# Attention loop on one Trainium2 core: the tile whose scores stay in PSUM is put first in each group of four, on TensorE and ScalarE

## The chip, the cores and the metric

The kernel runs on one core of a Trainium2 chip. The metric is the device time of one execution in microseconds (us); lower is better. The times below are the median of three executions. The profile and the trace come from one further execution, whose own time is given beside its span.

## The reference

Only the attention matters here. For four batches, sixteen heads, 1024 positions and a head dimension of 8:

```python
q, k, v = (heads(q), heads(k), heads(v))
scores = jnp.einsum('bhqd,bhkd->bhqk', q, k) * scale
scores = scores + _tisa_bias(amplitudes, sharpness, offsets, s)[None]
weights = jax.nn.softmax(scores, axis=-1)
attn = jnp.einsum('bhqk,bhkd->bhqd', weights, v)
out = attn.transpose(0, 2, 1, 3).reshape(b, s, d)
```

The bias depends on the head and on the distance between key and query, not on the batch. Ahead of it stand a layer norm and the projection to q, k and v; behind it a gated output projection, a residual, a second layer norm and a small feed-forward layer in 8-bit numbers.

## The kernel before

The attention is one loop over 8 pairs of heads (`Fori(0, NH2)`, index i). Each pass holds 16 **groups** g (2 heads times 8 blocks of 128 keys), written out one after the other. A group has four **tiles**, one for each batch b. A tile is 128 keys by 1024 queries of scores. So the loop has 128 groups, 512 tiles. Three engines share the work of a tile, and each runs its own instructions strictly in the order in which they are written; semaphores tie the engines together.

Names used from here on, for group g and tile b:

- **S_b** is the matmul pair (two halves of the queries) of the scores on TensorE, line 1043. For b = 0, 1, 2 the result lands in one of two pairs of PSUM banks, used in turn (`unit(k)`, with k = 3g + b counting these tiles). For b = 3 it lands in the one pair of banks 4 and 5.
- **T** follows S_3 alone: four matmuls (line 1052) add the bias to the scores where they lie in PSUM. Tile 3 is the tile that stays in PSUM; VectorE never touches it.
- **z_b** is VectorE's addition (line 1118), b = 0, 1, 2 only: PSUM plus bias, into a buffer in SBUF. It counts up `z_ready`.
- **e_b** is ScalarE's exponential (line 1170 for b = 0, 1, 2, in place in the SBUF buffer; line 1178 for b = 3, from PSUM to the buffer). It counts up `p_ready`.
- **P0 and P1** are TensorE's products of the group's four exponentials with the values, one for each half of the queries (line 1068; each shows as 8 matmul records, two passes over four column strips).

Who waits for whom: z_b waits for S_b; S_b of the tiles 0 to 2 waits until the addition two tiles earlier has emptied its banks (`z_ready` at k - 1); e_b waits for z_b, e_3 for T. P0 of group g waits for all four exponentials of g. S_3 of group g waits, before the change, for `p_ready` at 4 g, which is all four exponentials of group g - 1. TensorE computes scores two groups ahead of the products (`LAG = 2`), four sets of SBUF buffers hold the groups in flight, and the order in which TensorE takes the pieces of one step is a table in the loop:

```python
for steps, c in (((0,), 0), ((1,), 1), ((2, 3), None)):
    ...
        for b in steps:
            scores(i, g + LAG, b)
    ...
    if c is not None:
        products(i, g, c)
```

So in step g TensorE runs S_0 of group g + 2, P0 of g, S_1 of g + 2, P1 of g, S_2 and S_3 with T of g + 2. ScalarE takes the tiles of each group in the order 0, 1, 2, 3. Once in each pass of the head pairs, in group 1, VectorE and ScalarE each also copy one half of the finished output out of PSUM (lines 400 and 401), and in group 3 VectorE takes a reciprocal.

Of the kernel before, what the change touches and what calls it, by code (L numbers as in the profile page):

```python
# [30 lines left out]
B, S, D = 4, 1024, 128  # L31
# [29 lines left out]
ROW = 64  # L61
ROW2 = 16
EARLY = (H - 2) * HD
PAIR = 2
RING = [2, 3, 4, 5, 6, 7]
NLN = 5
# [2 lines left out]
def attention_block(nc, io, out):  # L69
    with ExitStack() as ctx:  # L70
# [22 lines left out]
        win = sb("win", [P, 3 * D], F32)  # L93
        wgate = sb("wgate", [EARLY + 1, 2 * D], F32)
        wlast = sb("wlast", [P, 2 * D], F32)
# [296 lines left out]
        p_ready = sem("p_ready")  # L392
        num_in = [sem(f"num_in{b}") for b in range(B)]

        GPH = TB
# [34 lines left out]
        def gate_main(eng, i):  # L430
# [3 lines left out]
            if i >= len(RING):  # L434
                eng.wait_ge(prod_ready, i - len(RING) + 1)
            for m in range(PAIR):
                t = PAIR * o + m
                eng.matmul(gate_ps(i)[:, m * 2 * D:(m + 1) * 2 * D], num[b][0:EARLY + 1, t * P:(t + 1) * P],  # L438
                           wgate[:, :], start=(m == 0), stop=True, skip_group_check=True)
# [15 lines left out]
        with nc.Block() as block:  # L455
            @block.sync
            def _(eng):
# [8 lines left out]
                eng.dma_start(wffn[:, :], io["w_ffn"]).then_inc(consts_in, 16)  # L466
                eng.dma_start(wgate[0:EARLY, :], io["w_gate"][0:EARLY, :]).then_inc(consts_in, 16)
                eng.dma_start(wgate[EARLY:EARLY + 1, :], io["b_gate"].rearrange("(a n) -> a n", a=1)).then_inc(consts_in, 16)
                for b in range(B):
                    eng.dma_start(wlast[32 * b:32 * b + 2 * HD, :], io["w_gate"][EARLY:P, :]).then_inc(consts_in, 16)  # L470
                with nc.allow_non_contiguous_dma(reason="128 biases, one per partition"):
# [475 lines left out]
            def _(eng):  # L947
# [29 lines left out]
                with eng.Fori(0, NH2) as i:  # L977
# [13 lines left out]
                    with eng.If(i > NH2 - 2):  # L991
# [3 lines left out]
                        for b in range(B):  # L995
                            eng.dma_start(num[b][0:EARLY, :], o_dram[b, 0:H - 2]).then_inc(num_in[b], 16)
                            eng.dma_start(num[b][EARLY:EARLY + 1, :], rd[HD + 1:HD + 2, :]).then_inc(num_in[b], 16)
# [24 lines left out]
            @block.tensor  # L1022
            def _(eng):
                def scores(i, g, b):

                    p, t = (g // GPH) % 2, g % GPH
                    by_vector = b < DPG
                    if b == 0 and t == 0:
                        eng.wait_ge(head_in[p], (i + (g // (2 * GPH))) * (16 * LOADS) + 16 * LOADS)
                    if by_vector:  # L1030
                        k = DPG * g + b
                        u = unit(k)

                        if k >= 2:
                            eng.wait_ge(z_ready, i * (2 * DPH) + (k - 1))
                    else:
                        u = 4
                        if g:
                            eng.wait_ge(p_ready, i * (8 * GPH) + 4 * g)
                    keys = slice(b * S + t * P, b * S + (t + 1) * P)  # L1040
                    for c in range(2):
                        rows = slice(ROW * c, ROW * c + 33)
                        last = eng.matmul(ps[:, u + c, :], kb[p][rows, keys],  # L1043
                                          qb[p][rows, b * HALF:(b + 1) * HALF],
                                          start=True, stop=True)
                    if by_vector:
                        last.then_inc(sd_ready, 1)
                        return
                    for c in range(2):
                        for m in range(2):  # L1050
                            c0 = t * P + 64 * m + c * HALF
                            last = eng.matmul(ps[64 * m:64 * m + 64, u + c, :], ident2[:, :],  # L1052
                                              t64[p][:, c0:c0 + HALF], start=False, stop=True,
                                              skip_group_check=True)
                    last.then_inc(sp_ready, 1)

                def products(i, g, c):

                    p, t = (g // GPH) % 2, g % GPH
                    if c == 0:  # L1060
                        eng.wait_ge(p_ready, i * (8 * GPH) + 4 * (g + 1))
                        if t == 0:
                            eng.wait_ge(vst_in, i * 2 + (p + 1))
                    if t == 0 and p == 0:

                        eng.wait_ge(o_ready[c], i + 1)
                    for b in range(B):
                        last = eng.matmul(ps[32 * b:32 * b + 32, 6 + c, :], vst[p][:, b * TB + t, :],  # L1068
                                          slot(g, b)[:, c * HALF:(c + 1) * HALF],
                                          start=(t == 0 and p == 0), stop=(t == TB - 1 and p == 1))  # L1070
                    if c == 1:
                        last.then_inc(groups_done, 1)
                    elif t == TB - 1 and p == 1:
                        last.then_inc(half_done, 1)

                eng.wait_ge(consts_in, 16 * 9)
                eng.wait_ge(fk_ready, B - 1)
                eng.wait_ge(fk_last, 1)
                eng.wait_ge(fq_ready, B)
                for g in range(LAG):  # L1080
                    for b in range(B):
                        if g == 0 and b == 1:
                            eng.wait_ge(v_copied, B)
                        scores(0, g, b)
                with eng.Fori(0, NH2) as i:
                    for g in range(2 * GPH):

                        for steps, c in (((0,), 0), ((1,), 1), ((2, 3), None)):
                            if g < 2 * GPH - LAG:
                                for b in steps:  # L1090
                                    scores(i, g + LAG, b)
                            else:

                                with eng.If(i < NH2 - 1):
                                    for b in steps:
                                        scores(i, g + LAG, b)
                            if g == 2 * GPH - 1 and c == 0:

                                with eng.If(i > NH2 - 2):
                                    eng.wait_ge(z_ready, NH2 * 2 * DPH)  # L1100
                                    gate_main(eng, 0)
                            if c is not None:
                                products(i, g, c)
# [56 lines left out]
            @block.scalar  # L1160
            def _(eng):
                eng.wait_ge(norm_ready, 2)
                eng.wait_ge(consts_in, 16 * 9)
                with eng.Fori(0, NH2) as i:
                    for g in range(2 * GPH):
                        for b in range(B):
                            buf = slot(g, b)
                            if b < DPG:
                                eng.wait_ge(z_ready, i * (2 * DPH) + (DPG * g + b + 1))
                                eng.activation(buf, buf, ACT.Exp).then_inc(p_ready, 1)  # L1170
                            else:
                                if g == SETS // 2:

                                    eng.wait_ge(qk_out, 16 * 4 * B)
                                eng.wait_ge(sp_ready, i * (2 * GPH) + (g + 1))

                                eng.wait_ge(groups_done, i * (2 * GPH) + (g + 1))
                                eng.activation(buf, banks(4, 2), ACT.Exp).then_inc(p_ready, 1)  # L1178
                            if b == 0 and g == LAG - 1:

                                with eng.If(i > 0):
                                    eng.wait_ge(groups_done, i * (2 * GPH) + SETS)
                                    eng.wait_ge(o_stored, i * (16 * 2 * B))
                                    copy_half(eng, 1).then_inc(o_ready[1], 1)
                eng.wait_ge(groups_done, H * GPH + SETS)
                eng.wait_ge(o_stored, NH2 * 16 * 2 * B)
                copy_half(eng, 1).then_inc(o_ready[1], 1)


            NP = NT // PAIR  # L1190
            PB = NP // B
            LN = [slice(0, 8), slice(8, 16), slice(16, 24), slice(24, 28), slice(28, 32)]
            LN_LAST = [g.stop // PAIR - 1 for g in LN]
            LN_VECTOR = [2, 2, 3, 2, 2]
# [13 lines left out]
            def pair_tile(i):  # L1208

                return (i % B) * TB + PAIR * (i // B)  # L1210

# [432 lines left out]
```

## Time and profile before

| | us |
|---|---|
| median of 3 executions | 596.91 (596.88 to 600.4) |
| profiled execution, its own time | 598.76 |
| profiled execution, span | 595.8 |
| mean granted TensorE clock | 0.972 of full speed |

The span runs from the first to the last instruction; the time measured on the device adds what lies around it, 2.96 us here. The loop over the head pairs takes from about 51 to 539 us of the span.

### The profile page before, as it was taken

How to read it: one execution, taken by the hardware profiler on the slowest of the kernel's cores; microseconds unless marked ns; L12 is line 12 of the kernel's file. 1: busy time of each engine (PE TensorE's matmuls, PEld its weight loads, DVE VectorE, ACT ScalarE, POOL GpSimd, SP SyncE). 2: the span in 40 equal slices, each digit the busy share in tenths (PEclk: the TensorE clock that was granted, in tenths of full speed). 3: DMA queues.
4: the chain of work that ended last, by engine and by line, in shares of the span. 5: the costliest groups of instructions: out<-in, count | busy, mean ns of one | idle time of the engine just before them, and what ended most of it. 6: DMA issues, size and time to landing. Idle time of an engine off the chain costs nothing.

```text
span 595.8 us, 12699 instructions
## 1 busy us (share of the span) xinstructions
PE 570.1 (96%) x4093; PEld 160.2 (27%) x4093; DVE 548.3 (92%) x672; ACT 549.6 (92%) x609; POOL 71.5 (12%) x89
## 2 busy tenths in 40 slices
PE   9998999999999999999999999999999999999654
PEld 4643122222222222222222222222222222226532
DVE  5966999999999999999999999999999999995985
ACT  5858999999999999999999999999999999993673
POOL 6274000001000100010001000100001000101810
PEclk9998999999999999999999999999999999999857
DMA  7443505051505150415041504150325132410004
GB/s 183 148 152 110 147 10 152 5 148 36 155 8 143 34 155 14 138 38 154 17 136 39 149 22 128 47 146 25 119 57 135 36 112 64 113 29 0 2 0 141
DMA packets 29387, 51.35 MB, mean 86 GB/s; under 512 B 9425, under 2 KB 20858, under 8 KB 28410
## 3 DMA queue, kind: packets, MB, share of 16 engines
q1 hardware_dynamic: 27482, 50.61, 30.2%
q10 hardware_dynamic: 1888, 0.53, 0.4%
q8 instruction: 8, 0.13, 0.1%
q14 instruction: 9, 0.07, 0.1%
HBM read 42.13 MB, written 8.75 MB: 85 GB/s over the span
## 4 chain that ended last, share of the span: by engine, by line
ACT 37%; issue 35%; PE 22%; DVE 5%; ACTq 1%; DVEq 0%; POOL 0%; POOLq 0%
ACT pbuf L1170 16%; ACT split L1170 15%; PE ps L1068 5%; PE ps L1043 3%; ACT pbuf L1178 2%; ACT split L1178 2%; PE ps L835 2%; PE ps L438 2%; PE ps L1052 1%; PE ps L769 1%; PE ps L746 1%; PE ps L754 1%; PE ps L1390 1%; DVE x_sb L1593 1%; DVE split L1534 1%
## 5 line engine op out<-in xcount | busy, mean ns | idle before, releaser
L1118 DVE TENSOR_TENSOR split<-ps,t 128x1024 f32<-128x1024 f32 x192 | 233.5, 1224 | 10.8 <-PE ps L1043 5.3
L1118 DVE TENSOR_TENSOR pbuf<-ps,t 128x1024 f32<-128x1024 f32 x192 | 231.1, 1221 | 7.2 <-PE ps L1043 2.5
L1170 ACT ACTIVATE pbuf<-pbuf 128x1024 f32<-128x1024 f32 x192 | 204.0, 1254 | 0.8 <-DVE pbuf L1118 0.7
L1170 ACT ACTIVATE split<-split 128x1024 f32<-128x1024 f32 x192 | 202.0, 1261 | 1.5 <-DVE split L1118 1.5
L1043 PE MATMUL ps<-qb,kb 33*128 33x512 f16 x1024 | 182.4, 388 | 4.9 <-ACT pbuf L1178 2.6
L1068 PE MATMUL ps<-pbuf,vst 128*32 128x512 f32 x1024 | 137.2, 608 | 0.0
L1068 PE MATMUL ps<-split,vst 128*32 128x512 f32 x1024 | 136.0, 604 | 0.0
L1043 PEld LDWEIGHTS ps<-qb,kb 33*128 33x128 f16 x1024 | 48.6, 92 | 289.7 <-DVE pbuf L1118 110.7
L1052 PE MATMUL ps<-t64s,ident 128*64 128x512 f16 x512 | 80.1, 393 | 0.0
L1178 ACT ACTIVATE split<-ps 128x1024 f32<-128x1024 f32 x64 | 78.3, 1223 | 0.0
L1178 ACT ACTIVATE pbuf<-ps 128x1024 f32<-128x1024 f32 x64 | 77.8, 1215 | 0.0
L303 POOL COPY vst<-v_all 128x256 f32 (+1 forms) x16 | 6.4, 399 | 262.2 <-PE ps L1068 250.7
L1017 POOL TENSOR_TENSOR o_sbs<-o_sbs,rd 128x1024 f32<-128x1024 f32 x7 | 16.7, 2383 | 175.8 <-DMA rd<-r_scratch 175.8
L1068 PEld LDWEIGHTS ps<-split,vst 128*32 128x32 f32 x1024 | 20.3, 108 | 30.0 <-issue 29.7
L1068 PEld LDWEIGHTS ps<-pbuf,vst 128*32 128x32 f32 x1024 | 20.2, 108 | 29.4 <-issue 29.4
L1052 PEld LDWEIGHTS ps<-t64s,ident 128*64 128x64 f16 x512 | 18.1, 108 | 30.8 <-issue 30.8
L438 PE MATMUL ps<-wgate,v_all 113*128 113x256 f32 x64 | 15.2, 386 | 0.0
L1362 PE MATMUL ps<-ident,split 128*128 128x128 f32 x32 | 6.9, 387 | 7.9 <-ACT split L1434 4.5
L835 PE MATMUL ps<-zeros 128*128 128x512 f16 x45 | 12.7, 450 | 1.1 <-POOL zeros L496 1.1
L1298 POOL TENSOR_TENSOR x_sb<-x_sb,pbuf 128x256 f32<-128x256 f32 x12 | 8.7, 756 | 38.5 <-DVE pbuf L1501 38.5
L438 PEld LDWEIGHTS ps<-wgate,v_all 113*128 113x128 f32 x64 | 11.7, 190 | 3.2 <-issue 1.8
L635 DVE BATCH_NORM_STATS2 stats<-x_sb 128x6 f32<-128x128 f32 x32 | 6.5, 277 | 5.6 <-DMA x_sb<-in_L_attn_x 5.6
(163 smaller groups left out, 300.6 us busy)
## 6 DMA issues: line engine op xcount, KB each, us to landing
t<-g_scratch SPq DMA_DIRECT2D x15, 960.0 KB
kb<-k_scratch SPq DMA_DIRECT2D x120, 64.0 KB
t64s<-gh_scratch SPq DMA_DIRECT2D x16, 248.0 KB
t64s<-gl_scratch SPq DMA_DIRECT2D x16, 248.0 KB
qb<-q_scratch SPq DMA_DIRECT2D x60, 64.0 KB
x_sb<-in_L_attn_x SPq DMA_DIRECT2D x4, 512.0 KB, 7.7
q_scratch<-split SPq DMA_DIRECT2D x8, 256.0 KB, 2.7
k_scratch<-split SPq DMA_DIRECT2D x8, 256.0 KB, 2.6
```

What stands on the lines that cost most here:

```text
L438: eng.matmul(gate_ps(i)[:, m * 2 * D:(m + 1) * 2 * D], num[b][0:EARLY + 1, t * P:(t + 1) * P], wgate[:, :], start=(m == 0), stop=True, ski ...
L635: last = eng.bn_stats(stats[:, n, :], x_sb[:, n, :])
L835: eng.matmul(ps[:, 7, :], zeros[:, 0:P], zeros[:, :], start=True, stop=True)
L1017: eng.tensor_tensor(o_sb, o_sb, rd[:, :], ALU.mult).then_inc(o_norm, 1)
L1043: last = eng.matmul(ps[:, u + c, :], kb[p][rows, keys], qb[p][rows, b * HALF:(b + 1) * HALF], start=True, stop=True)
L1052: last = eng.matmul(ps[64 * m:64 * m + 64, u + c, :], ident2[:, :], t64[p][:, c0:c0 + HALF], start=False, stop=True, skip_group_check=True)
L1068: last = eng.matmul(ps[32 * b:32 * b + 32, 6 + c, :], vst[p][:, b * TB + t, :], slot(g, b)[:, c * HALF:(c + 1) * HALF], start=(t == 0 and ...
L1118: eng.tensor_tensor(slot(g, b), banks(unit(k), 2), t128[p][:, t * P:t * P + S], ALU.add).then_inc(z_ready, 1)
L1170: eng.activation(buf, buf, ACT.Exp).then_inc(p_ready, 1)
L1178: eng.activation(buf, banks(4, 2), ACT.Exp).then_inc(p_ready, 1)
L1298: eng.tensor_tensor(xs, xs, gate[:, j % NG, :], ALU.add).then_inc(x1_ready, 1)
L1362: last = eng.transpose(turn_ps(g)[:, m * P:(m + 1) * P], xn2[:, n, :], ident[:, :])
```

## The change

In each group the tile 3 comes first, then 0, 1, 2, on TensorE (the start-up and the loop) and on ScalarE. VectorE keeps its order 0, 1, 2. S_3 of group g now waits for `p_ready` at 4 g - 3 in place of 4 g: since e_3 is now the first exponential of its group, this is the count that e_3 of group g - 1 brings. The wait for a new head's loads moves to the tile that comes first.

```diff
+ORDER = (3, 0, 1, 2)
...
-                    if b == 0 and t == 0:
+                    if b == ORDER[0] and t == 0:
                         eng.wait_ge(head_in[p], (i + (g // (2 * GPH))) * (16 * LOADS) + 16 * LOADS)
...
                         if g:
-                            eng.wait_ge(p_ready, i * (8 * GPH) + 4 * g)
+                            eng.wait_ge(p_ready, i * (8 * GPH) + (4 * g - 3))
...
                 for g in range(LAG):
-                    for b in range(B):
+                    for b in ORDER:
...
-                        for steps, c in (((0,), 0), ((1,), 1), ((2, 3), None)):
+                        for steps, c in (((3,), 0), ((0,), 1), ((1, 2), None)):
...
                     for g in range(2 * GPH):
-                        for b in range(B):
+                        for b in ORDER:
                             buf = slot(g, b)
```

TensorE in the loop before, one step: S_0, P0, S_1, P1, S_2, S_3 with T, and S_0 of the next step. The rows name the operation and its tiles; REGISTER_ALU rows compute a semaphore's value for the wait behind them.

```order
L1043 MATMUL ps<-qb0,kb0 128x512 x2
L1068 MATMUL ps<-pbuf,vst0 32x512 x4
L1035 REGISTER_ALU
L1043 MATMUL ps<-qb0,kb0 128x512 x2
L1068 MATMUL ps<-pbuf,vst0 32x512 x4
L1035 REGISTER_ALU
L1043 MATMUL ps<-qb0,kb0 128x512 x2
L1039 REGISTER_ALU
L1043 MATMUL ps<-qb0,kb0 128x512 x2
L1052 MATMUL ps<-t64s,ident2 64x512 x4
L1035 REGISTER_ALU
L1043 MATMUL ps<-qb0,kb0 128x512 x2
```

The same place after the change (lines are one higher), one step: S_3 with T, P0, S_0, P1, S_1, S_2, and S_3 with T of the next step.

```order
L1044 MATMUL ps<-qb0,kb0 128x512 x2
L1053 MATMUL ps<-t64s,ident2 64x512 x4
L1062 REGISTER_ALU
L1069 MATMUL ps<-pbuf,vst0 32x512 x4
L1036 REGISTER_ALU
L1044 MATMUL ps<-qb0,kb0 128x512 x2
L1069 MATMUL ps<-pbuf,vst0 32x512 x4
L1036 REGISTER_ALU
L1044 MATMUL ps<-qb0,kb0 128x512 x2
L1036 REGISTER_ALU
L1044 MATMUL ps<-qb0,kb0 128x512 x2
```

P0 stood behind S_0; it now stands behind T, so that between S_3's wait and the next S_0 there lies P0 where there was nothing.

ScalarE in the loop before, around the border between two groups (the buffers of one group are in `pbuf`, of the next in `split`):

```order
L1170 ACTIVATE pbuf<-pbuf 128x1024
L1175 REGISTER_ALU
L1178 ACTIVATE pbuf<-ps 128x1024
L1169 REGISTER_ALU
L1170 ACTIVATE split<-split 128x1024
```

The same border after the change:

```order
L1171 ACTIVATE pbuf<-pbuf 128x1024
L1176 REGISTER_ALU
L1179 ACTIVATE split<-ps 128x1024
L1170 REGISTER_ALU
L1171 ACTIVATE split<-split 128x1024
```

The exponential that reads PSUM follows e_2 in both, but it was the same group's and is now the next group's.

## Rows read from the trace of the kernel before

**Rows 1.** The page: busy time, share of the span, instructions of each engine

```profile
PE 570.1 (96%) x4093; PEld 160.2 (27%) x4093; DVE 548.3 (92%) x672; ACT 549.6 (92%) x609; POOL 71.5 (12%) x89
```

**Rows 2.** Stretches: PE, PEld, DVE, ACT, POOL busy, granted clock, DMA

```profile
50.00:54.30 4.30, 2.90 (x21) 1.02 (x19) 3.17 (x3) 2.86 (x3) 2.31 (x3) 1.00 0.05 14
54.30:61.10 6.80, 5.64 (x22) 0.91 (x22) 4.94 (x5) 6.72 (x8) 5.30 (x7) 0.50 0.00 1
...
100.00:532.00 432.00, 429.64 (x3204) 95.88 (x3206) 419.69 (x358) 432.00 (x465) 22.16 (x21) 1.00 0.30 83
```

**Rows 3.** Timeline of TensorE, one step: start, us, operation, count

```profile
202.72 0.39 PE L1043 MATMUL ps<-qb,kb 33*128 33x512 f16 x2
203.04 1.06 PE L1068 MATMUL ps<-split,vst 128*32 128x512 f32 x8
204.03 0.39 PE L1043 MATMUL ps<-qb,kb 33*128 33x512 f16 x2
204.35 1.06 PE L1068 MATMUL ps<-split,vst 128*32 128x512 f32 x8
205.35 0.63 PE L1043 MATMUL ps<-qb,kb 33*128 33x512 f16 x4
205.91 0.62 PE L1052 MATMUL ps<-t64s,ident 128*64 128x512 f16 x4
206.47 0.39 PE L1043 MATMUL ps<-qb,kb 33*128 33x512 f16 x2
```

**Rows 4.** Timeline of VectorE and ScalarE beside it

```profile
205.79 1.23 DVE L1118 TENSOR_TENSOR pbuf<-ps,t 128x1024 f32<-128x1024 f32 x1
...
204.31 1.23 ACT L1178 ACTIVATE split<-ps 128x1024 f32<-128x1024 f32 x1
205.21 3.16 ACT L1170 ACTIVATE pbuf<-pbuf 128x1024 f32<-128x1024 f32 x3
208.06 1.23 ACT L1178 ACTIVATE pbuf<-ps 128x1024 f32<-128x1024 f32 x1
```

**Rows 5.** Timeline around the output copies of pass i = 4

```profile
298.63 0.68 DVE L400 COPY o_sbs<-ps 128x512 f32<-128x512 f32 x1
299.23 2.35 DVE L1118 TENSOR_TENSOR pbuf<-ps,t 128x1024 f32<-128x1024 f32 x2
...
300.36 0.86 ACT L401 ACTIVATE o_sbs<-ps 128x512 f32<-128x512 f32 x1
300.84 2.28 ACT L1170 ACTIVATE pbuf<-pbuf 128x1024 f32<-128x1024 f32 x2
...
302.73 1.30 ACT L1178 ACTIVATE pbuf<-ps 128x1024 f32<-128x1024 f32 x1
303.35 0.39 PE L1043 MATMUL ps<-qb,kb 33*128 33x512 f16 x2
304.08 0.39 PE L1043 MATMUL ps<-qb,kb 33*128 33x512 f16 x2 [0.34 <-ACT pbuf L1178]
304.40 0.62 PE L1052 MATMUL ps<-t64s,ident 128*64 128x512 f16 x4
304.96 0.39 PE L1043 MATMUL ps<-qb,kb 33*128 33x512 f16 x2
...
305.48 1.23 DVE L1118 TENSOR_TENSOR split<-ps,t 128x1024 f32<-128x1024 f32 x1 [0.47 <-PE ps L1043]
```

**Rows 6.** Waits from 64 to 534 us: us in total, times, longest

```profile
PE ps L1043 <- ACT pbuf L1178: 2.4, 7, 0.3
```

**Rows 7.** Timeline of the start of the loop, where TensorE waits

```profile
53.41 1.22 DVE L1118 TENSOR_TENSOR pbuf<-ps,t 128x1024 f32<-128x1024 f32 x1
...
54.68 0.61 PE L1043 MATMUL ps<-qb,kb 33*128 33x512 f16 x2 [0.74 <-DVE pbuf L1118]
...
54.65 1.06 ACT L1170 ACTIVATE pbuf<-pbuf 128x1024 f32<-128x1024 f32 x1
55.62 1.01 ACT L1178 ACTIVATE pbuf<-ps 128x1024 f32<-128x1024 f32 x1
...
56.68 0.60 PE L1043 MATMUL ps<-qb,kb 33*128 33x512 f16 x2 [0.26 <-ACT pbuf L1178]
58.21 0.10 PEld L1043 LDWEIGHTS ps<-qb,kb 33*128 33x128 f16 x2 [0.81 <-DVE pbuf L1118]
58.75 1.94 PE L1068 MATMUL ps<-pbuf,vst 128*32 128x512 f32 x8
```

## Prediction

> **What bounds the kernel now.** I read the page's busy shares first: TensorE 96%, VectorE 92%, ScalarE 92% [rows 1]. Between 100 and 532 us, which is the loop alone, they are 429.64, 419.69 and 432.00 of 432 us, at the full granted clock [rows 2]. Such shares do not say who sets the pace, since a record's length holds time in which its engine already runs the next one. So I read starts. The reader is to see in the TensorE timeline that one step, from S_0 to the next S_0, takes 206.47 - 202.72 = 3.75 us, and that no wait is noted on its matmuls [rows 3]. ScalarE's four exponentials also start 208.06 - 204.31 = 3.75 us apart: 0.90 us from e_3 to e_0 and (208.06 - 205.21) / 3 = 0.95 from each of the others to the next [rows 4], which is ScalarE at its own pace. VectorE can start an addition every 2.35 - 1.22 = 1.13 us when its scores are there [rows 5], 3.39 us for three; it starts z_2 0.44 us after S_2 [rows 3, 4] and so waits for TensorE. TensorE and ScalarE are level, VectorE has 0.36 us to spare.
>
> The list of waits in the loop gives TensorE one real stall in each pass of the head pairs, 7 in all, for e_3 [rows 6]. In pass 4 it lies at 303.35: S_3 comes 0.73 us after S_2, where 205.91 - 205.35 - 0.32 = 0.24 us is usual, so 0.49 us are lost [rows 3, 5]. It comes from ScalarE's output copy. A pass is therefore 16 x 3.75 + 0.49 = 60.49 us.
>
> **What the change does to each engine's own work.** On TensorE nothing is added. From S_3 to the end of T is 304.96 - 304.08 = 0.88 us, P0 is 204.03 - 203.04 = 0.99, S and P together 1.32 (204.03 to 205.35), and S before another S 0.24 [rows 3, 5]. The new step is 0.88 + 0.99 + 1.32 + 2 x 0.24 = 3.67 us, 0.08 less than now. One term is not in the trace: P behind T. S before T (304.08 to 304.40) and S before P (202.72 to 203.04) both take 0.32 [rows 3, 5], and so does the last pair of T before an S (304.40 to 304.96, less 0.24 for the first pair); I take 0.32, with the bounds 0.24 (S before S) and 0.53 (half of what a pass of P takes, 1.06, the longest step of that kind) [rows 3]. ScalarE's work stays 3.75 us, VectorE's 3.39. The new wait count by itself gives nothing: 4 g was the count of e_3 of group g - 1 in the old order, where e_3 was the last of its group, and 4 g - 3 is the count of the same exponential now.
>
> **What the change does to the loop of waits.** Here is the price. S_3 of group g + 2 waits for e_3 of group g + 1. ScalarE reaches that one right behind e_2 of group g, which needs z_2 of group g. Before, S_3 was the last of TensorE's step, and the next S_0 followed it in 0.88 us. Now P0 stands between them. Follow it from S_0 of group g at time 0:
>
> - S_1 starts at 1.32, behind P1 [rows 3]; z_1 0.44 later at 1.76 [rows 3, 4]; z_2 1.13 later at 2.89 [rows 5]; it ends 1.22 later at 4.11.
> - From the end of an addition z_2 through its exponential and the one from PSUM to the S_3 that waited for it: the start of the loop shows just this chain with nothing else in the way. The addition ends at 53.41 + 1.22 = 54.63, the exponentials start at 54.65 and 55.62, S_3 at 56.68. That is 2.05 us [rows 7]. S_3 starts at 6.16.
> - From S_3 through T (0.88) and P0 (0.99) to S_0 of group g + 2: 1.87 us, at 8.03 [rows 3, 5].
>
> So two groups take 8.03 us, one 4.015. The same sum before is 4.11 + 2.05 + 0.88 = 7.04 us for two, 3.52 for one: it had 0.23 us to spare below the 3.75 of TensorE, and P0 in the circle uses that up and more. Each of the some 126 groups behind the first two costs 4.015 - 3.75 = 0.265 us, 33.4 us together. ScalarE, at 3.75, and TensorE, at 3.67, then both idle some 0.3 us in a group.
>
> **A second circle**, shorter: S_0 to z_0 is 305.48 - 304.96 = 0.52 us, the addition 1.23, the release of the banks to TensorE 0.05 (54.63 to 54.68) [rows 5, 7]. S_2, which needs them, can start at 1.80 where TensorE would reach it at 1.56; then 0.24 to S_3 and 1.87 to S_0: 3.91 us. TensorE used to space the tiles 0, 1, 2 evenly; now 0.24 us lie between S_1 and S_2, and 2.1 us between S_2 and S_0. This circle hides under the first, but stays if the first is cheaper than I think.
>
> **Once in a pass.** VectorE's output copy sets z_1 0.60 us back (298.63 to 299.23) [rows 5]. z_0 could be followed by z_1 at 0.52 + 1.13 = 1.65, and z_1 is wanted at 1.76, so 0.11 is covered and 0.49 goes into the circle. ScalarE's copy (0.48, from 300.36 to 300.84 [rows 5]) lies behind e_0, where ScalarE waits for the late z_1; the reciprocal lies where VectorE idles. The old stall of 0.49 goes, the new one is 0.49: nothing on balance, and a pass is 16 x 4.015 + 0.49 = 64.7 us.
>
> **Start and end.** P0 of group 0 now stands ahead of S_0 of group 2, at the low granted clock, 1.94 us for both its passes instead of 1.06 [rows 3, 7], while VectorE has run dry. S_0 waited for an addition there (58.21) and covers some of it: an estimate of 1.5 us. At the end the last exponential before the last products is e_2, not e_3 behind it, which gives back 0.95 [rows 4]. Together 0.6 us.
>
> **The sum.** 33.4 + 0 + 0.6 = 34 us. On the profiled execution's own 598.76 us that is 632.8, on the median of 596.91, 1.85 us lower, it is **631 us**, 5.7% slower.
>
> **The bounds.** P behind T at 0.24 takes 0.04 us from each group, 5 us; at 0.53 it adds 0.105, 13 us. The 2.05 us were read where ScalarE started fresh. Where it runs full, e_3 is recorded at 1.30 us, not 1.01 [rows 5, 7]; if that length counts in the circle, it adds 0.145 to a group, 18 us. So 626 to 649. I stay with the fresh value, since ScalarE will wait for z_2 in each group.
>
> **The rivals.**
> *The first circle is not closed* (ScalarE gets ahead, so that S_3's exponential is ready sooner) and the second sets the pace: 126 x (3.91 - 3.75) = 20 us and the start's 0.6, some 618 us. For it: the first circle is the sum of eight readings, and 0.2 us too much over two groups is enough. Against: the order of every engine is fixed, and e_3 cannot pass e_2. Chance 0.12.
> *Neither closes, not slower than before*: the gain of 0.08 us on TensorE leads, and ScalarE, at 16 x 3.75 + 0.48 for its copy, bounds the pass at 60.48: 596 to 597 us. It decides this way if z_2 to S_3 takes at most 2.05 - (8.03 - 7.50) = 1.52 us, less than the 0.97 + 1.01 us of the two exponentials alone [rows 7]. Else TensorE would have to run P0 while S_3 waits; at the one place where S_3 waits, 303.35 to 304.08, nothing that is written behind it ran ahead [rows 5]. Chance 0.06.
> *The clock falls.* TensorE will pause twice in each group. In the trace the granted clock fell from full to half (2.4 to 1.2 GHz) behind 50.00 to 54.30, where TensorE was busy 2.90 of 4.30 us, 67%; in the loop it stayed full at 99%, and the forecast has 3.67 / 4.015, 91%, which no row shows [rows 2]. At half, P takes 1.94 for 1.06 [rows 3, 7], so a step takes about 6.7 us, and with half of the loop there it would be 64 x (6.7 - 4.0), 170 us more than my forecast: some 800. Chance 0.03.
> The Trainium skill, "TensorE: Matmul & The Clock Gate", section "A second HAM failure mode: psum-queue depth-cycling", tells of a kernel whose small pauses between groups of matmuls, from cycling through PSUM banks, made the clock swing between its levels. It speaks for this last rival; the trace of before has such small gaps only at the copies, and its clock held there [rows 2, 5].
>
> **How the numbers follow.** The forecast with its bounds has 0.79, of it 0.12 in the part above 640. The range 617 to 645 takes in the second circle and the bounds but for the last microseconds of the dearest. A measurement of this kernel can tell about 1% from no change. Slower by over 1%: 0.79 + 0.12 + 0.03 = 0.94; within 1%: 0.05; faster: 0.01.
>
> **What would show it.** Right: starts of S_0 4.0 us apart; the list of waits with TensorE on e_3 (from PSUM) and on VectorE's additions about once in each group, 0.2 to 0.3 us each; ScalarE's records near 1.06 us, not 1.26 (3.16 less two steps of 0.95 [rows 4]); VectorE idle between groups. Wrong, if the S_0 are 3.9 apart and only waits on additions are left, if they are 3.75 apart, or if the granted clock shows 0.5 in the loop.

## The result, and the profile after

| | before | after |
|---|---|---|
| median | 596.89 us (596.49 to 600.4, 4 runs) | 630.41 us (629.79 to 631.1, 4 runs) |
| ratio | | 1.055, 95% interval 1.0528 to 1.0572 |
| profiled execution, span | 595.8 us | 629.2 us |
| mean granted clock | 0.972 | 0.974 |

The change costs 33.5 us; 34 were forecast. One of the twelve executions of experiment 6 below took 878.8 us at a mean granted clock of 0.555; ratios leave it out.

The page's busy shares after, against [rows 1]:

```profile
PE 587.4 (93%) x4093; PEld 160.6 (26%) x4093; DVE 543.0 (86%) x672; ACT 570.5 (91%) x609; POOL 71.6 (11%) x89
```

The work is the same (the same number of records on each engine), and each engine covers a smaller share of a longer span. Busy time is no measure of work here: ScalarE's grew from 549.6 to 570.5 us and TensorE's from 570.1 to 587.4 us, although neither does more. Before, ScalarE's records of about 1.26 us overlapped, since a new one starts every 0.95 us; now they last about 1.05 us, and only part of the free time shows as time without a record. In the loop (columns as in [rows 2]) the clock is still full:

```profile
100.00:560.00 460.00, 442.73 (x3186) 95.11 (x3180) 412.47 (x356) 448.71 (x463) 22.23 (x21) 1.00 0.28 79
```

The timeline of TensorE, over two steps, answers to [rows 3]; lines are one higher than before:

```profile
327.54 0.39 PE L1044 MATMUL ps<-qb,kb 33*128 33x512 f16 x2
...
331.69 0.39 PE L1044 MATMUL ps<-qb,kb 33*128 33x512 f16 x2
332.01 1.06 PE L1069 MATMUL ps<-split,vst 128*32 128x512 f32 x8
333.00 1.09 PE L1044 MATMUL ps<-qb,kb 33*128 33x512 f16 x6
334.03 0.62 PE L1053 MATMUL ps<-t64s,ident 128*64 128x512 f16 x4
334.58 1.07 PE L1069 MATMUL ps<-pbuf,vst 128*32 128x512 f32 x8
335.58 0.39 PE L1044 MATMUL ps<-qb,kb 33*128 33x512 f16 x2
335.90 1.06 PE L1069 MATMUL ps<-pbuf,vst 128*32 128x512 f32 x8
336.89 1.34 PE L1044 MATMUL ps<-qb,kb 33*128 33x512 f16 x6
338.17 0.62 PE L1053 MATMUL ps<-t64s,ident 128*64 128x512 f16 x4
```

S_0 starts at 327.54, 331.69 and 335.58: groups of 4.15 and 3.89 us, 8.04 for two. Most groups of the loop alternate in this way. What differs is the stretch of six score matmuls, S_1, S_2 and S_3, up to T: 334.03 - 333.00 = 1.03 us in the short step and 338.17 - 336.89 = 1.28 in the long one, where 0.24 + 0.24 + 0.32 = 0.80 would be TensorE's own pace. So S_2 is held in each step, and in the long one S_3 besides. T to P0 takes 334.58 - 334.03 = 0.55 us, as T to S_0 did.

The chain that ended last shows the circle whole. Before, between 200 and 212 us, its work was ScalarE's alone ("issue" is time in which the engine waited for nothing that the profile shows):

```profile
by line: issue 56.1%; ACT pbuf L1170 25.3%; ACT split L1170 12.5%; ACT pbuf L1178 3.9%; ACT split L1178 3.8%; ACTq L1169 0.9%
```

After, it goes round all three engines:

```profile
328.75 1.02 ACT pbuf L1179
...
329.82 0.39 PE ps L1044 x2
330.21 0.55 PE ps L1053 x4
330.76 1.00 PE ps L1069 x8
331.75 0.32 PE ps L1044 x2
332.08 0.99 PE ps L1069 x8
333.07 0.34 PE ps L1044 x2
...
333.44 0.05 DVE pbuf L1119
...
334.58 1.23 DVE pbuf L1119
...
335.83 0.04 ACT pbuf L1171
...
336.79 1.01 ACT split L1179
```

From e_3 of one group through S_3, T, P0, S_0, P1, S_1, z_1, z_2 and e_2 to e_3 of the group after the next: 336.79 - 328.75 = 8.04 us. The reader is to see that each piece starts where the one before it ends, and that P0 (330.76) is among them.

The list of waits has rows for the weight loads ahead of the matmuls (PEld) too. Before, from 64 to 534 us:

```profile
PEld ps L1043 <- ACT pbuf L1178: 4.4, 7, 0.6
DVE split L1118 <- PE ps L1043: 3.3, 7, 0.5
```

After, from 64 to 565 us:

```profile
DVE split L1119 <- PE ps L1044: 26.1, 55, 0.8
DVE pbuf L1119 <- PE ps L1044: 24.7, 55, 0.6
PEld ps L1044 <- ACT split L1179: 15.1, 38, 0.6
PEld ps L1044 <- ACT pbuf L1179: 13.1, 37, 0.4
```

VectorE stands idle ahead of z_0 110 times, in nearly every one of the some 124 groups of this stretch, 50.8 us together, waiting for S_0, the scores that come late. TensorE waits for e_3 75 times in place of 7, in three groups of five.

The pass of the head pairs can be read from the starts of VectorE's output copy: the first is in pass 1, another in pass 4, the last behind the loop. Before, then after (the two times in the row are the first and the last start):

```profile
L400 DVE COPY o_sbs<-ps x8: 680/681/692, 117.2 to 539.2; 128x512 f32<-128x512 f32 x8
```

```profile
L401 DVE COPY o_sbs<-ps x8: 681/681/692, 122.5 to 572.5; 128x512 f32<-128x512 f32 x8
```

And from the timeline after, in pass 4:

```profile
316.78 0.68 DVE L401 COPY o_sbs<-ps 128x512 f32<-128x512 f32 x1
```

Before a pass takes (298.63 - 117.2) / 3 = 60.48 us with the copy of pass 4 at 298.63 [rows 5], after (316.78 - 122.5) / 3 = 64.76.

### The profile page after: what moved, and what is told of

Same layout as the page of the kernel before. It is cut to its first block, busy times and chain, and to the rows that moved or that the text cites. A ratio compares the mean times of both kernels' runs of the same rounds, so it can differ in the third digit from the quotient of the medians.

```text
span 629.2 us, 12811 instructions
## 1 busy us (share of the span) xinstructions
PE 587.4 (93%) x4093; PEld 160.6 (26%) x4093; DVE 543.0 (86%) x672; ACT 570.5 (91%) x609; POOL 71.6 (11%) x89
## 4 chain that ended last, share of the span: by engine, by line
PE 52%; DVE 18%; issue 17%; ACT 10%; DVEq 1%; ACTq 0%; POOL 0%; POOLq 0%
PE ps L1069 22%; PE ps L1044 13%; DVE pbuf L1119 8%; PE ps L1053 7%; DVE split L1119 6%; ACT split L1179 5%; ACT pbuf L1179 4%; PE ps L836 2%; PE ps L439 2%; PE ps L770 1%; PE ps L747 1%; PE ps L755 1%; PE ps L1391 1%; DVE x_sb L1594 1%; PE ps L737 1%
## 5 line engine op out<-in xcount | busy, mean ns | idle before, releaser
L1119 DVE TENSOR_TENSOR split<-ps,t 128x1024 f32<-128x1024 f32 x192 | 229.2, 1221 | 29.6 <-PE ps L1044 29.0
L1119 DVE TENSOR_TENSOR pbuf<-ps,t 128x1024 f32<-128x1024 f32 x192 | 228.4, 1219 | 28.3 <-PE ps L1044 28.1
L1044 PE MATMUL ps<-qb,kb 33*128 33x512 f16 x1024 | 190.9, 387 | 20.9 <-ACT split L1179 2.3
L1171 ACT ACTIVATE split<-split 128x1024 f32<-128x1024 f32 x192 | 198.2, 1052 | 8.1 <-DVE split L1119 2.7
L1171 ACT ACTIVATE pbuf<-pbuf 128x1024 f32<-128x1024 f32 x192 | 199.2, 1053 | 6.7 <-DVE pbuf L1119 0.6
L1179 ACT ACTIVATE split<-ps 128x1024 f32<-128x1024 f32 x64 | 64.4, 1007 | 0.0
L1179 ACT ACTIVATE pbuf<-ps 128x1024 f32<-128x1024 f32 x64 | 64.4, 1006 | 0.0
L523 POOL TENSOR_TENSOR pbuf<-split 128x1024 bf16<-128x1024 f16 x6 | 11.2, 1894 | 2.9 <-DVE pbuf L648 2.9
```

Of the source, the lines that this page charges most:

```text
L523: eng.tensor_tensor(sq[b][:, i, :], part, part, ALU.mult).then_inc(sq_ready, 1)
L1044: last = eng.matmul(ps[:, u + c, :], kb[p][rows, keys], qb[p][rows, b * HALF:(b + 1) * HALF], start=True, stop=True)
L1119: eng.tensor_tensor(slot(g, b), banks(unit(k), 2), t128[p][:, t * P:t * P + S], ALU.add).then_inc(z_ready, 1)
```

## The experiments

The first four are edits of the changed kernel and are compared with the same runs of the kernel before (597.0 us). The last four are compared with another set (597.18); 5 edits the kernel before, 8 the changed one, 6 and 7 the kernels of experiments 1 and 3.

**1. P0 behind S_0.**

```diff
-                        for steps, c in (((3,), 0), ((0,), 1), ((1, 2), None)):
+                        for steps, c in (((3, 0), 0), ((1,), 1), ((2,), None)):
```

> The changed kernel with one edit: in each step P0 moves behind S_0 (S_3 with T, S_0, P0, S_1, P1, S_2). ScalarE's order and the new wait stay. My theory (the loss is P0 in the circle S_0, z_1, z_2, e_2, e_3, S_3, S_0): the circle falls from 8.03 us for two groups to 8.03 - 0.99 = 7.04, 3.52 for one, below TensorE's own 3.75; a pass is 60.4 to 60.5 us, the time 595 to 597 us, S_0 3.75 us apart. Rival A (the loss is ScalarE's order or the looser wait itself): it stays near 630. Rival B (the price is P behind T on TensorE, not a wait): also 597, but then the record after the change would have shown a step above 3.67 without waits.

Measured: 596.98 us, ratio to before 0.9996 (0.9977 to 1.0015). The timeline of TensorE:

```profile
324.75 0.39 PE L1044 MATMUL ps<-qb,kb 33*128 33x512 f16 x2
325.07 1.06 PE L1069 MATMUL ps<-split,vst 128*32 128x512 f32 x8
...
328.50 0.39 PE L1044 MATMUL ps<-qb,kb 33*128 33x512 f16 x2
```

S_0 is 3.75 us apart again; the waits on TensorE's own list are the 7 for e_3, once in a pass, 2.4 us as before, and a pass takes (299.68 - 118.2) / 3 = 60.49 us by the starts of the output copies. Tile 3 is still first on both engines and the wait is the new one, so neither of them costs anything that these runs can tell (the interval is 0.2% to each side); rival A falls. The whole 33.4 us (630.41 - 596.98) hang on P0 standing between S_3 and S_0. Rival B falls on the record after the change, where T to P0 takes 0.55 us, what T to S_0 took before.

**2. TensorE's order alone**, with ScalarE's old order and the old wait.

```diff
-                            eng.wait_ge(p_ready, i * (8 * GPH) + (4 * g - 3))
+                            eng.wait_ge(p_ready, i * (8 * GPH) + 4 * g)
...
-                        for b in ORDER:
+                        for b in range(B):
                             buf = slot(g, b)
```

> The changed kernel's TensorE order with ScalarE's old order (tiles 0, 1, 2, 3) and the old wait (all four exponentials of the group before). My theory: the same circle is now closed within one group, since e_3 of group g follows e_2 of group g and S_3 of g + 1 stands ahead of P0 and S_0 of g + 1: 4.11 + 2.05 + 1.87 = 8.03 us for one group instead of two, 127 x (8.03 - 3.75) = 544 us more than before, about 1140 us at the full granted clock. TensorE would be busy only 46% of the time, so its clock may fall; with P at 1.94 us in place of 1.06 a group would take about 10.6 us, some 1470 us. Rival A (ScalarE's new order is what costs): it would be at 597 or little above. Rival C (only VectorE's banks, the second circle, matter): 3.9 us for a group, 618.

Measured: 1413.07 us (2 runs), ratio 2.366 (2.362 to 2.371), between the two times of the expectation and near the one at the low clock. The chain, from one e_3 to the next:

```profile
504.51 1.02 ACT pbuf L1179
...
505.57 0.61 PE ps L1044 x2
506.18 1.00 PE ps L1053 x4
507.18 1.87 PE ps L1069 x8
509.04 0.54 PE ps L1044 x2
509.58 1.45 PE ps L1069 x8
511.03 0.34 PE ps L1044 x2
...
512.54 1.23 DVE pbuf L1119
...
514.75 1.02 ACT pbuf L1179
```

The same circle in the same order, now closed within one group: 514.75 - 504.51 = 10.24 us. It is above the 8.03 because the granted clock fell, as the expectation allowed (columns as in [rows 2]):

```profile
505.60:508.00 2.40, 2.40 (x14) 0.46 (x14) 0.00 (x0) 0.00 (x0) 0.00 (x0) 0.50 0.00 0
...
510.00:510.90 0.90, 0.90 (x8) 0.00 (x0) 0.90 (x1) 0.00 (x0) 0.00 (x0) 0.73 0.00 0
510.90:511.60 0.70, 0.67 (x8) 0.13 (x4) 0.24 (x2) 0.63 (x1) 0.00 (x0) 1.00 0.00 0
511.60:515.80 4.20, 0.00 (x0) 0.00 (x0) 2.15 (x2) 3.45 (x4) 0.00 (x0) 0.77 0.00 0
505.57:515.81 10.24, 6.00 (x28) 0.92 (x29) 3.58 (x3) 4.08 (x4) 0.00 (x0) 0.67 0.00 0
```

P0 takes 1.87 us here, not 1.00. The parts on VectorE and ScalarE, from the end of S_1's piece at 511.37 to the end of e_3's at 515.77, are the 4.4 us that they are in the changed kernel (333.41 to 337.80). TensorE's pieces are longer than in the chain of the changed kernel: S_3 by 0.22 us, T by 0.45, P0 by 0.87, S_0 by 0.22, P1 by 0.46, together 2.22, and 10.24 - 8.04 is 2.20. So the clock is the whole difference between the two lengths. This also says what the pair of ScalarE's order and the new wait is for: with S_3 ahead of P0 and S_0 on TensorE, ScalarE must not leave e_3 to the end of its own group.

**3. ScalarE's order alone**, with TensorE's old order; the wait stays the new one.

```diff
-                    if b == ORDER[0] and t == 0:
+                    if b == 0 and t == 0:
...
-                    for b in ORDER:
+                    for b in range(B):
                         if g == 0 and b == 1:
...
-                        for steps, c in (((3,), 0), ((0,), 1), ((1, 2), None)):
+                        for steps, c in (((0,), 0), ((1,), 1), ((2, 3), None)):
```

> The changed kernel's ScalarE order (3, 0, 1, 2) and wait with TensorE's old order (S_0, P0, S_1, P1, S_2, S_3 with T). My theory: nothing of the loss is left. Circle: S_3 of g + 1 to the end of T 1.0, e_3 to the end of e_2 0.90 + 0.95 + 0.95 + 1.06 = 3.86, P0 to S_3 of g + 3 2.55 and the release 0.05, 7.46 us for two groups, 3.73 for one, just under TensorE's 3.75. 595 to 598 us. Rival A (the loss is ScalarE's order): near 630.

Measured: 601.73 us, ratio 1.0076 (1.0059 to 1.0093), nearly 4 us above the upper end of what I expected. The loss of the changed kernel is not there, but another one is. The timeline at the output copy of pass 4:

```profile
303.88 0.39 PE L1044 MATMUL ps<-qb,kb 33*128 33x512 f16 x2
304.37 0.63 ACT L402 ACTIVATE o_sbs<-ps 128x512 f32<-128x512 f32 x1
...
305.05 1.07 PE L1069 MATMUL ps<-pbuf,vst 128*32 128x512 f32 x8 [0.78 <-ACT o_sbs L402]
```

P1, the products of the second half, must not overwrite the banks before ScalarE has copied them out. In this order ScalarE starts e_3 of a group only when TensorE has brought S_3 at the end of its step, and so runs later behind the additions; the copy ends at 305.00, where P1 could have begun at 303.88 + 0.32 = 304.20, behind S_1. P1 starts at 305.05, 0.85 us late, and so it goes once in each pass (7 times in the list, up to 0.8 us). Of the 4.7 us lost, 8 x 0.48 = 3.8 lie in the passes; where the rest goes was not followed. My sum of the circle had left out this wait, `o_ready`. Experiment 7 tests it.

**4. e_3 of the next group between e_1 and e_2**, on ScalarE, with TensorE's order as after the change.

```diff
-                            eng.wait_ge(p_ready, i * (8 * GPH) + (4 * g - 3))
+                            eng.wait_ge(p_ready, i * (8 * GPH) + max(4 * g - 4, 1))
...
-                        eng.wait_ge(p_ready, i * (8 * GPH) + 4 * (g + 1))
+                        eng.wait_ge(p_ready, i * (8 * GPH) + (4 * (g + 1) + 1))
...
-                        for b in ORDER:
+                        for b in (0, 1, 3, 2):
...
+                            elif g < 2 * GPH - 1:
+                                exp_kept(i, g + 1)
```

`exp_kept` is the exponential of tile 3 with its waits. The second changed wait is that of P0: e_3 of the group after is now counted ahead of it.

> TensorE's order as after the change; ScalarE takes e_3 of the next group between e_1 and e_2 of this one, so e_3 no longer stands behind z_2 (at the very end of the last pass a tiny exponential of one column takes its place to keep the count). This opens the first circle (z_1 in place of z_2: 2.98 + 2.05 + 1.87 = 6.90 us for two groups) and leaves the second: S_0, z_0, S_2, S_3 with T, P0, S_0, 3.91 us by the rows of before, 3.89 by the short groups of after. My theory: groups 3.89 to 3.91 us apart, all alike, 126 x 0.15 = 19 us above before less the 3.4 us of its old stalls, 611 to 616 us. Rival (only the first circle exists): TensorE and ScalarE at 3.75, near 597. Rival (the cost is TensorE's order as such, whatever ScalarE does): near 630.

Measured: 613.57 us, ratio 1.0272 (1.0255 to 1.0289). The timeline of TensorE:

```profile
330.56 0.39 PE L1045 MATMUL ps<-qb,kb 33*128 33x512 f16 x2
...
334.44 0.39 PE L1045 MATMUL ps<-qb,kb 33*128 33x512 f16 x2
...
335.76 1.09 PE L1045 MATMUL ps<-qb,kb 33*128 33x512 f16 x6
...
338.33 0.39 PE L1045 MATMUL ps<-qb,kb 33*128 33x512 f16 x2
```

The groups are 3.89 us apart with the short stretch of 1.02 us (335.76 to 336.78) for the six score matmuls, except three in a pass around the output copies; the list of waits has no entry for e_3 on TensorE any more. A pass takes (308.62 - 120.8) / 3 = 62.61 us, which is 16 x 3.89 = 62.24 and 0.37 at the copies. So the second circle exists, and alone it costs half of the loss (16.6 of 33.5 us). Both rivals fall.

**5. The output copy given to VectorE**, on the kernel before.

```diff
-            if c == 0:
+            if c == 0 or vector:
...
+                            if b == DPG - 1 and g == LAG - 1:
+                                with eng.If(i > 0):
+                                    eng.wait_ge(groups_done, i * (2 * GPH) + SETS)
+                                    copy_half(eng, 1, vector=True).then_inc(o_ready[1], 1)
...
-                            if b == 0 and g == LAG - 1:
-
-                                with eng.If(i > 0):
-                                    eng.wait_ge(groups_done, i * (2 * GPH) + SETS)
-                                    eng.wait_ge(o_stored, i * (16 * 2 * B))
-                                    copy_half(eng, 1).then_inc(o_ready[1], 1)
```

> The kernel before, with ScalarE's output copy once in a pass given to VectorE, behind z_2 of group 1. The trace of before has a pass at 60.49 us, 0.49 of it TensorE's wait for the exponential that the copy delays, and VectorE has 0.36 us to spare in each group. My theory: the stall goes but for what VectorE's second copy delays itself; a pass 60.0 to 60.3 us, 593 to 596 us. Rival: VectorE's two copies, 1.2 us close together, run into the release of the banks for TensorE's next scores and cost as much, 597 to 600.

Measured: 598.1 us (594.7 to 598.61), ratio 0.9998 (0.9980 to 1.0016). The first copy of pass 1 starts at 117.0 and that of pass 4 at 297.86, a pass is 60.29 us, 0.2 less than before. That is 1.6 us in all. The list of waits has P1 waiting for the second copy in its place (1.6 us in 7 times, `PEld ps L1068 <- DVE o_sbs L400`). The pass is within what was expected, the median within the range of its rival: of these runs five are near 595 or 596 and seven near 598, and the trace is of one of the five (594.84). Inconclusive in the time; in the trace the stall went from 0.49 to 0.29 us.

**6. The same on the kernel of experiment 1.**

> The same move of the output copy to VectorE on the kernel with tile 3 first and P0 behind S_0. Since that kernel's circle and pass were those of before, my theory expects the same as for the kernel before with the copy moved, within 1 us: 593 to 596 us. Rival: with e_3 ahead of its group the copy had another place on ScalarE, so the gain differs by more than 1 us.

Measured: 596.47 us, ratio 0.9982 (0.9966 to 0.9999); copies in pass 1 at 118.4 and in pass 4 at 299.21, a pass of 60.27. The pass is that of experiment 5, as expected. The median is 0.5 us above the expected range and 1.6 below that of experiment 5, whose runs are split. Against before there is a gain of 0.2%, at the edge of what can be told.

**7. The same on the kernel of experiment 3.**

> ScalarE's order new, TensorE's old, and the output copy on VectorE. Without the move this order measured 601.7 us, where 595 to 598 was expected; its list of waits shows P1 waiting for ScalarE's output copy 7 times, 0.8 us each, since ScalarE runs some 2.3 us later behind the additions in this order. If that is the cause, the move takes it away: 594 to 598 us. If the 4.7 us come from e_2 as the last of the group before P0 (its list shows 100 short waits there), they stay, 600 to 602.

Measured: 595.49 us, ratio 0.9967 (0.9949 to 0.9985). The copies of passes 1 and 4 are at 117.8 and 298.10: a pass is 60.10 us, where experiment 3 had (300.27 - 117.4) / 3 = 60.96. The difference of 0.86 us is the 0.85 by which P1 came late there, so the output copy was the cause of the loss; the short waits of P0 for e_2 are still in the list, 109 of up to 0.3 us, and do not cost it. The time is 0.3% below that of the kernel before; against experiment 6 it can't be told apart. TensorE's own 16 x 3.75 = 60.0 is nearly reached.

**8. Half of T left out**, as a dose, on the changed kernel. It leaves out the bias of tile 3 for half of the queries.

```diff
-                    for c in range(2):
+                    for c in range(1, 2):
                         for m in range(2):
                             c0 = t * P + 64 * m + c * HALF
```

> The changed kernel with half of T: the bias is added to tile 3 only for the second half of the queries, one of two pairs of matmuls, 0.24 us, left out (so the bias of tile 3's first half is missing). A dose for the first circle: 8.03 - 0.24 = 7.79 us for two groups, 3.895 for one, and the second falls to 3.89 - 0.24 = 3.65, out of play. My theory: 126 x 0.12 = 15 us below the changed kernel, about 615 us. Rival (the second circle alone sets the pace): a full 0.24 in each group, 600. Rival (ScalarE or VectorE set it, T lies beside them): no change, 630.

Measured: 617.52 us, ratio to before 1.0341 (1.0307 to 1.0374), 12.9 us below the changed kernel's 630.41, where 15 were expected and 30 or 0 by the rivals. The timeline of TensorE:

```profile
324.71 0.39 PE L1044 MATMUL ps<-qb,kb 33*128 33x512 f16 x2
...
328.51 0.39 PE L1044 MATMUL ps<-qb,kb 33*128 33x512 f16 x2
...
332.53 0.39 PE L1044 MATMUL ps<-qb,kb 33*128 33x512 f16 x2
```

Two groups take 332.53 - 324.71 = 7.82 us, 0.22 less than 8.04. A piece of 0.24 us taken out of every group shortens two groups by one such piece, not by two: the circle passes through T once in two groups. How the two share the time does not matter: here the groups are 3.80 and 4.02 us.

## Why the prediction was right

**The first circle** was put at 8.03 us for two groups from rows of the kernel before (it speaks of eight readings; the sum has seven terms); it measures 8.04. Its parts hold one by one: S_0 to z_2 2.89 (331.69 to 334.58), S_3 to S_0 1.87 (329.82 to 331.69), e_3's start to S_3 1.07 (1.06 in [rows 7]), z_2 to e_2 to e_3 2.21 (334.58 to 336.79). To read the exponentials where ScalarE starts fresh was right: the page has them at 1.05 and 1.01 us, not at 1.26 and 1.22; the bound of 649 fell with that. P behind T was taken at 0.32 us and is 0.31 (0.55 less 0.24). The condition of the rival "not slower", z_2's end to S_3 in at most 1.52 us, failed: the chain has 334.58 + 1.23 = 335.81 to 336.79 + 1.07 = 337.86, 2.05 as forecast.

**One sum of it was wrong**, without effect on the forecast: the circle before. The prediction puts z_2 at 2.89 us behind S_0 there too, but in the old order S_2 stands behind P1, and z_2 starts at 205.79 - 202.72 = 3.07 [rows 3, 4]. So it is 3.07 + 1.22 + 2.05 + 0.88 = 7.22 us for two groups, 3.61 for one, and it had 0.14 us to spare below 3.75, not 0.23. Experiment 1 has the same order from S_0 on, so its expectation, 3.52, is to be read as 3.61; both are below 3.75.

**The second circle** was put at 3.91 us and measures 3.89, alone in experiment 4. That came out at 613.57 where the prediction's rival gave 618. Of the 0.44 us by which a pass (62.61) is below the rival's 16 x 3.91 + 0.49 = 63.05, 0.32 are the 3.89 for 3.91 and 0.12 the copies. The expectation of experiment 4 took off all 3.4 us of the old stalls, where 0.37 us stayed in a pass; its range was wide enough for that.

**What I had not seen** is how the two circles share the time. I expected each group at 4.0 us, with the second circle hidden under the first. In fact both close. The first one fixes only what two groups take together, and the second fixes the least that one can take: after a short group of 3.89 the next gets the rest, 4.15. Near the border of two passes the split is another: z_0 starts at 307.61, 311.61 and 315.64, which is 4.00 and 4.03, and the sum is the same. So the forecast of the time did not need the split, but the sign to look for, a wait for e_3 about once in each group, did not come: the list has 75 in some 124 groups.

**Once in a pass** the new stall was put at 0.49 us, a pass at 64.7; it measures 64.76, which leaves 64.76 - 8 x 8.04 = 0.4 us for it.

**Start and end** were mis-sized, and the sign of their sum was wrong: +0.6 us forecast. The first output copy comes 122.5 - 117.2 = 5.3 us later. Of these, 15 groups behind the first two, at 4.28 / 16 = 0.27 us each, make 4.0, so the start costs 1.3, not 1.5. From the copy in pass 7 to the one behind the loop (six passes after the first) it was 539.2 - 117.2 - 6 x 60.48 = 59.1 us and is 572.5 - 122.5 - 6 x 64.76 = 61.4; another 15 groups would add 4.0, so the end gives back 1.7, not 0.95. Why it gives back more is open. Together start and end are -0.4. The three parts, 5.3 + 6 x 4.28 + 2.3, make 33.3 of the 33.4 us by which the spans differ; the 126 groups give 33.7 of them where 33.4 was forecast. That the total is met within 0.5 us is in part luck, since the two errors, +0.3 and -1.0, offset each other.

**The rival "not slower"** otherwise needed products that run ahead of a waiting S_3. Nothing of the kind is in the chain. **The clock** held at 1.00 in the loop (100 to 560 us). It did fall in experiment 2, where TensorE was busy 6.00 of 10.24 us; so the rival's mechanism is real in this loop, but not at the size of the pauses that the change makes.

## What to carry to other kernels

When instructions of several in-order engines are reordered, count the circle, not the queue: follow one wait round through every engine back to its start, add what stands between on each, and divide by the number of groups that it spans. An engine can have less work of its own in a group, as TensorE does here (3.75 to 3.67 us by the prediction's sum), and the loop still lose, because a long independent piece (P0, 0.99 us) slipped between a wait and the instruction that the others wait for. Keep such a piece out of the circle: behind S_0 instead of ahead of it, the same new order cost nothing (ratio 0.9996).

## What the runs showed of the hardware

In experiment 2 the groups are 10.24 us long where 8.03 would be their length at the full clock. TensorE was granted half the clock from the start of its work at 505.57 until about 510.5, the full clock from there, through the end of P1, S_1, S_2 and the first two microseconds of the pause, which starts at 511.6, and half the clock again from about 513.9. So the full clock came late in the group, and more than half of it fell into the pause: 0.50, 0.73 and 1.00 in the stretches with work, 0.77 in the pause, 0.67 in the mean. In each stretch looked at between 100 and 1200 us the mean is 0.67 too.

The length of ScalarE's records tells how full it is: the same exponential is 1.26 us where the engine runs without a gap and 1.05 where it starts fresh, although from one start to the next it takes 0.95 us in the first case and 0.97 in the second [rows 4, 7].
